# Two residual sums move from ScalarE and VectorE to VectorE alone, and their shifts into 32 columns

## The chip, the cores and the metric

The kernel runs on one core of one Trainium2 chip. The metric is device time in microseconds (us) from one launch to its end; lower is better.

## The reference

Eight layers in a row act on x of shape (8, 512, 128) in float32. Each layer has the form x = x + LN(layer(LN(x))), where LN takes mean and variance over the 128 channels of one token and has no weights. What matters here is the end of the sequence:

```python
x = x + _layernorm(_L2_ffn_ref(_layernorm(x), ...))    # expert choice
x = x + _layernorm(_L3_attn_ref(_layernorm(x), ...))   # rotary attention, 16 heads of 8
x = x + _layernorm(_L3_ffn_ref(_layernorm(x), ...))    # mixture of up to 4 experts
return x

def _layernorm(x, axis=-1, eps=1e-05):
    m = jnp.mean(x, axis=axis, keepdims=True)
    v = jnp.var(x, axis=axis, keepdims=True)
    return (x - m) / jnp.sqrt(v + eps)
```

LN of an output o is o times a scale plus a shift, where scale = 1/sqrt(var + eps) and shift = -mean times scale. Both are one number for each token. Adding one number to all 128 channels of a token doesn't change LN of that token.

## The kernel before

The 4096 tokens lie as 32 tiles of 128 tokens: a token is a partition, its 128 channels lie along the free axis. `c.x` holds the running sum, `c.n` the normalised input of the next layer, `c.o` the output of the last one. Four tiles make one of the 8 batches (`TPB` = 4, `B` = 8). The stages follow each other in the program (`program`), each a block with one instruction stream for each engine; the order within a stream is written out by hand, and engines wait for each other on semaphores.

A normalisation is an object of class `LayerNorm` with four steps, each of one batch:

- `spread` on VectorE (DVE): four BN_STATS (L2505) and four BN_AGGR (L2508) give mean and variance.
- `factors` on GpSimd (POOL): variance plus eps (L2514), minus the mean (L2515), the power -1/2 (L2517), the shift (L2520). Where the object has `late`, one more addition puts `c.late` on top of the shift (L2522, L2524).
- `apply` or `apply_tile` on ScalarE (ACT): one activation for each tile, scale times source plus shift (L2543, L2536).
- `add` on DVE: one SCALAR_TENSOR_TENSOR for each tile, x + o times scale, without the shift (L2530).

`c.late` is 32 columns, one for each tile. The stage before expert choice (linear attention) adds its two residuals by `add` and leaves the sum of the two shifts in `c.late`; the last normalisation of the mixture, `of_y`, adds it to its own shift, so the final x gets it.

The residual in front of a layer comes in two stages. In the rotary attention (`attention_layer` with `tables`, so `rope` is true) DVE runs `o_spread(b)`, POOL `of_o.factors`, ACT `of_o.apply` in place on `c.o`, and DVE `add(b)`, one TENSOR_TENSOR over 128x512 (L919). Then `x_spread(b)`, `of_x.factors` and `of_x.apply` give `c.n`. The mixture (`elastic_mixture`) does the same: `of_o.spread`, `of_o.factors`, `of_o.apply`, and `first_norm(b)` with its TENSOR_TENSOR (L2699) and the spread of x.

The attention's opening does batches 0 to 2 before the main loop. DVE: spreads of o(0) and o(1), `add(0)`, spread of x(0), weights copied, a memset (L985), spread of o(2), `add(1)`, spread of x(1), `add(2)`, spread of x(2), then two exchanges (STREAM_SHUFFLE, L931) and the splitting of queries into three bf16 parts (L509 to L515), which POOL does for the keys. ACT: `of_o.apply` of 0 and 1, `of_x.apply(0)`, copies `copy_tokens` (L814) and `keep` (L823), `of_o.apply(2)`, `of_x.apply(1)`, further copies. `keep(1, n)` waits for the parts of batch 0. POOL has the factors of o(0), o(1), x(0), two memsets (L646, L648), then the factors of o(2) and x(1).

The main loop has 32 quads of heads (i), each with four steps (k). In a step PE makes four score tiles (L740), the values of the step before (L750, eight matmuls), and two tiles for the row maxima (L727); ACT takes four exponentials (L839) and DVE two maxima (L942), from PSUM in both cases. Four quads belong to one batch (r = i mod 4), and the work for later batches is laid beside them: `of_x.apply_tile` at steps 1 to 4 of a batch, `of_o.apply_tile` at steps 5 to 8, `o_spread` on DVE at (r, k) = (0, 2), `add` at (2, 2), `x_spread` at (3, 2). PE makes keys at (2, 3) and values at (3, 3). These additions run for the five batches 3 to 7, on groups 0 to 4 of four quads.

In the mixture PE works through 32 pairs of batch and expert, `up` (L2608) and `down` (L2620); ACT does relu (L2656) and the two or three applies, DVE gathers (L2741).

Of the kernel before, what the change touches and what calls it, by code (L numbers as in the profile page):

```python
# [8 lines left out]
ALU = mybir.AluOpType  # L9
AX = mybir.AxisListType  # L10

B, S, D = 8, 512, 128
# [384 lines left out]
def attention_layer(c, tag, w, scale, tables=None, reload=None):  # L397
# [119 lines left out]
    with nc.Block() as block:  # L517
# [68 lines left out]
        def _(pool):  # L586
# [79 lines left out]
            for i in range(QUADS):  # L666
# [19 lines left out]
                if i + 2 < QUADS:  # L686
                    split_max(i + 2)

        @block.tensor
# [121 lines left out]
        def _(act):  # L811
# [45 lines left out]

            if rope:
                of_o.apply(act, c.o, c.o, 0)
                of_o.apply(act, c.o, c.o, 1)  # L860
            of_x.apply(act, c.n, c.x, 0)
            copy_tokens(0)
            keep(0, 0)
            keep(0, 1)
            if rope:
                of_o.apply(act, c.o, c.o, 2)
            of_x.apply(act, c.n, c.x, 1)
# [9 lines left out]
            for i in range(QUADS):  # L877
                b = i // TPB + AHEAD
                for k in range(4):
                    exps(i, k)  # L880
                    if k == 1 and i < LAST:
                        rows(i + 1)
                    at = 4 * (i % TPB) + k
                    if b < B and 1 <= at <= 4:
                        of_x.apply_tile(act, c.n, c.x, TPB * b + at - 1)
                    if rope and b + 1 < B and 5 <= at <= 8:
                        of_o.apply_tile(act, c.o, c.o, TPB * b + at - 1)
                    if b < B and at == 6:
                        copy_tokens(b)
                    if b < B and at == 7:  # L890
                        keep(b, 0)
                    if b < B and at == 11:
                        keep(b, 1)
                    if b < B and at == 15:
                        keep_values(b)

        @block.vector
        def _(dve):
# [18 lines left out]
            def add(b):  # L917
                dve.wait_ge(of_o.normed, TPB * (b + 1))
                nc.vector.tensor_tensor(batch_rows(c.x, b), batch_rows(c.x, b), batch_rows(c.o, b), ALU.add).then_inc(summed, 1)  # L919

            def x_spread(b):
                if rope:
                    dve.wait_ge(summed, b + 1)
                of_x.spread(dve, c.x, b)
# [1622 lines left out]
def elastic_mixture(c, d, small, out):  # L2547
# [15 lines left out]
    w1_in, w2_in, b1_turned, b1_copied = sem("w1_in"), sem("w2_in"), sem("b1_turned"), sem("b1_copied")  # L2563
    o_added, y_added, stored = sem("o_added"), sem("y_added"), sem("stored")
    turned, copied, gated, u_done, w_step, w_done = (sem(s) for s in ("turned", "copied", "gated", "u_done", "w_step", "w_done"))
# [5 lines left out]
    with nc.Block() as block:  # L2571
# [69 lines left out]
        def _(act):  # L2641
# [18 lines left out]
            nc.scalar.activation(b1T, c.bank(1)[:, 0:MIX * CHUNKS], ACT.Copy).then_inc(b1_copied, 1)  # L2660
            of_o.apply(act, c.o, c.o, 0)
            of_x.apply(act, c.n, c.x, 0)
# [4 lines left out]
            for g in range(STEPS):  # L2667
                b, e = divmod(g, MIX)
                if g + 1 < STEPS:
                    relu(g + 1)  # L2670
                if b + 1 < B and e == 0:
                    of_o.apply(act, c.o, c.o, b + 1)
                if b >= 1 and e == 0:
# [9 lines left out]
        @block.gpsimd  # L2683
        def _(pool):
            of_o.factors(pool, 0)
            of_x.factors(pool, 0)
            for b in range(B):
                if b >= 1:
                    of_y.factors(pool, b - 1)
                if b + 1 < B:  # L2690
                    of_o.factors(pool, b + 1)
                    of_x.factors(pool, b + 1)
            of_y.factors(pool, B - 1)

        @block.vector
        def _(dve):
# [4 lines left out]
            def first_norm(b):  # L2701
                residual(of_o, b, o_added)
                dve.wait_ge(o_added, b + 1)
                of_x.spread(dve, c.x, b)
# [160 lines left out]
```

## Time and profile before

| what | value |
|---|---|
| median of 3 runs | 2046.47 us |
| the 3 runs | 2046.47, 2047.84, 2041.81 us |
| the profiled execution, its own time | 2041.99 us |
| its span, first to last instruction | 2040.3 us |
| outside the span | 1.7 us |
| mean granted TensorE clock | 0.824 of 2.4 GHz |
| busy, of the span | PE 77%, DVE 60%, ACT 52%, POOL 39% |

In a row, a time is us from the start of the span; "x4" is the number of instructions; the part in brackets at the end is the engine's idle time just before and what ended it. Busy shares of the whole span are a mean over ten stages with different limits.

### The profile page before, as it was taken

Reading aid. Unit: us, or ns where it says so; the run is one execution under the profiler, and the core shown is the slowest. Engines: PE = TensorE matmul, PEld = TensorE weight load, DVE = VectorE, ACT = ScalarE, POOL = GpSimd, SP = SyncE. Lnnn points to the kernel's source line nnn. Section 1 sums busy time; section 2 is a strip of 40 time slices with the busy share of each in tenths; the row PEclk is TensorE's granted clock in tenths of the full one; section 3 lists DMA queues with packets and bytes.
Section 4 is the critical chain, followed back from the end, with each engine's and each line's share of the span. In section 5 each row is a group of like instructions: output and inputs, shape, how many; then the busy total and the mean of one; then the engine's idle time right before and its main releaser. Section 6 shows DMA issues by size and latency. Waiting matters only on the chain. (4 is left out here: it accounts for less than half of the span.)

```text
span 2040.3 us, 25722 instructions
## 1 busy us (share of the span) xinstructions
PE 1580.5 (77%) x8391; PEld 826.9 (41%) x8391; DVE 1224.0 (60%) x2794; ACT 1069.7 (52%) x2129; POOL 800.5 (39%) x1497
## 2 busy tenths in 40 slices
PE   2899999992659885074772595289999999789998
PEld 1133333320436554063662463123333333367776
DVE  3788888875743323004656750778888888334553
ACT  2377777774333333034663331257777777545553
POOL 3455555416243333515634376614444431011220
PEclk7699999996755555596765698579999999989999
DMA  4122222200000002100004122211111111000000
GB/s 117 66 66 66 65 67 64 64 14 1 1 0 1 0 1 88 54 28 10 3 1 129 55 39 30 90 48 60 61 62 59 61 64 45 26 18 11 11 6 16
DMA packets 84968, 85.16 MB, mean 42 GB/s; under 512 B 35942, under 2 KB 67536, under 8 KB 84708
## 3 DMA queue, kind: packets, MB, share of 16 engines
q1 hardware_dynamic: 73914, 75.14, 11.4%
q0 software_dynamic: 7680, 6.06, 1.8%
q10 hardware_dynamic: 3242, 2.32, 0.4%
q8 instruction: 67, 1.10, 0.2%
q14 instruction: 65, 0.53, 0.1%
HBM read 59.76 MB, written 25.17 MB: 42 GB/s over the span
## 5 line engine op out<-in xcount | busy, mean ns | idle before, releaser
L942 DVE TENSOR_REDUCE arena<-psum 128x2 f32<-128x1024 f32 x512 | 601.6, 1216 | 102.8 <-PE psum L727 98.3
L839 ACT ACTIVATE arena<-psum 128x512 f32<-128x512 f32 x1024 | 553.5, 595 | 135.4 <-PE psum L740 127.4
L727 PE MATMUL psum<-arena 72*128 72x512 bf16 x1024 | 287.8, 397 | 46.4 <-DMA arena<-L_k_parts 17.8
L740 PE MATMUL psum<-arena 99*128 99x512 bf16 x1024 | 312.0, 386 | 10.6 <-issue 7.1
L750 PE MATMUL psum<-arena 128*32 128x512 f32 x2048 | 274.5, 608 | 3.0 <-ACT arena L839 1.9
L2543 ACT ACTIVATE arena<-arena 128x128 f32<-128x128 f32 x316 | 128.6, 481 | 133.5 <-POOL arena L2520 121.3
L740 PEld LDWEIGHTS psum<-arena 99*128 99x128 bf16 x1024 | 74.6, 98 | 287.5 <-ACT arena L839 222.1
L2514 POOL TENSOR_SCALAR arena<-arena 128x4 f32<-128x4 f32 x112 | 30.6, 273 | 368.7 <-DVE arena L2508 363.2
L727 PEld LDWEIGHTS psum<-arena 72*128 72x128 bf16 x1024 | 95.3, 99 | 189.9 <-DVE arena L942 29.0
L2505 DVE BATCH_NORM_STATS2 arena<-arena 128x6 f32<-128x128 f32 x448 | 96.7, 278 | 75.9 <-PEq L101 21.0
L636 POOL TENSOR_TENSOR arena<-arena 128x16 bf16<-128x16 f32 x64 | 14.3, 223 | 290.8 <-DVE arena L942 218.4
L2656 ACT ACTIVATE arena<-psum,arena 128x512 f32<-128x512 f32 x128 | 84.3, 682 | 77.3 <-PE psum L2608 75.3
L627 POOL COPY arena<-arena 72x1024 f32<-72x1024 f32 x64 | 64.6, 1037 | 146.7 <-PE psum L740 126.5
L2620 PEld LDWEIGHTS psum<-arena 128*128 128x128 f32 x1024 | 118.1, 192 | 8.2 <-issue 8.2
L2517 POOL TENSOR_TENSOR arena<-arena 128x4 f32<-128x4 f32 x112 | 116.5, 1040 | 9.3
L2620 PE MATMUL psum<-arena 128*128 128x128 f32 x1024 | 119.9, 275 | 0.0
L2608 PE MATMUL psum<-arena 128*128 128x512 f32 x256 | 117.1, 601 | 0.0
L2741 DVE SCALAR_TENSOR_TENSOR arena<-psum,arena 128x128 f32<-128x128 f32 x128 | 36.0, 343 | 127.3 <-PE psum L2620 126.6
L750 PEld LDWEIGHTS psum<-arena 128*32 128x32 f32 x2048 | 40.4, 108 | 110.8 <-ACT arena L839 60.7
L2608 PEld LDWEIGHTS psum<-arena 128*128 128x128 f32 x256 | 46.9, 193 | 47.8 <-issue 47.8
L1741 POOL DMA_INDIRECT arena<-sw_rows_out,arena x32 | 33.2, 1037 | 67.8 <-SPq L1782 57.2
L1820 PE MATMUL psum<-arena 128*128 128x128 f32 x64 | 15.6, 392 | 55.3 <-ACT arena L2543 55.3
(433 smaller groups left out, 2532.2 us busy)
## 6 DMA issues: line engine op xcount, KB each, us to landing
arena<-L_q_parts SPq DMA_DIRECT2D x192, 96.0 KB
arena<-L_k_parts SPq DMA_DIRECT2D x180, 96.0 KB
L_q_parts<-arena SPq DMA_DIRECT2D x16, 384.0 KB, 3.4
L_k_parts<-arena SPq DMA_DIRECT2D x16, 384.0 KB, 3.3
arena<-in_L_ffn_w SPq DMA_DIRECT2D x1, 2048.0 KB, 10.6
ec_result<-arena SPq DMA_DIRECT2D x1, 2048.0 KB, 9.7
arena<-in_L_ffn_fc2s SPq DMA_DIRECT2D x1, 2048.0 KB, 16.1
ec_normed<-arena SPq DMA_DIRECT2D x2, 1024.0 KB, 7.3
```

Of the source, the lines that this page charges most:

```text
L627: nc.gpsimd.tensor_copy(rows[0:QK_ROWS, i % RING, :].rearrange("p (g j l) -> p g j l", g=4, j=HEADS), raw[0:QK_ROWS, i % RAW, :].rearrange ...
L727: last = nc.tensor.matmul(bank[:, 512 * h:512 * h + 512], columns(q9[0:QK_ROWS], i, m // 2, 128 * (2 * (m % 2) + h), 128), columns(k9[0:QK ...
L740: nc.tensor.matmul(acts.bank(name), columns(k9[0:ROWS], i, g, 128 * k, 128), columns(q9[0:ROWS], i, g, 0, 512), start=True, stop=True).the ...
L750: last = nc.tensor.matmul(out_bank[32 * g:32 * g + 32, :], v32[:, i % 2, g, k, :], prob[:, k % 2, g, :], start=(k == 0), stop=(k == 3))
L839: nc.scalar.activation(prob[:, k % 2, g, :], acts.bank(name), ACT.Exp, scale=scale).then_inc(act_taken, 1)
L942: nc.vector.tensor_reduce(neg_max[:, i % 2, 2 * m:2 * m + 2], maxes.bank(("max", i, m)).rearrange("p (h t) -> p h t", h=2), axis=AX.X, op= ...
L2505: self.nc.vector.bn_stats(self.stats[:, t, :], src[:, t, :]).then_inc(self.stats_done, 1)
L2517: self.nc.gpsimd.tensor_tensor(self.scale[:, at], self.var_eps[:, at], self.minus_half[:, 0:TPB], ALU.pow).then_inc(self.scale_done, 1)
L2543: self.nc.scalar.activation(dst[:, t, :], src[:, t, :], ACT.Identity, bias=self.shift[:, t:t + 1], scale=self.scale[:, t:t + 1]).then_inc( ...
L2608: nc.tensor.matmul(c.bank(k), w1[:, e, 128 * k:128 * k + 128], c.nT[:, b, 1:S + 1], start=True, stop=True).then_inc(h_made, 1)
L2620: last = nc.tensor.matmul(c.bank(4 + g % 2)[:, 128 * t:128 * t + 128], hT[:, g % 2, k, 128 * t:128 * t + 128], w2[:, e, k, :], start=(k == ...
L2656: nc.scalar.activation(hT[:, g % 2, k, :], c.bank(k), ACT.Relu, bias=b1T[:, CHUNKS * e + k:CHUNKS * e + k + 1]).then_inc(h_done, 1)
```

## The change

ACT no longer applies `of_o` in the rotary attention or the mixture. DVE's `add(b)` becomes `of_o.add`: four SCALAR_TENSOR_TENSOR of 128x128 in place of one TENSOR_TENSOR of 128x512, and it waits for POOL's factors where it waited for ACT. `c.x` then lacks the shift of that residual. POOL adds the shifts to `c.late`: once over 32 columns at the end of the attention, and in the mixture over 4 columns for each batch (`o_factors`, with a semaphore that `y_factors` waits for), ahead of the factors of `of_y`.

```diff
+            if rope:
+                pool.wait_ge(of_o.factors_done, B)
+                nc.gpsimd.tensor_tensor(c.late, c.late, of_o.shift, ALU.add)
...
-            if rope:
-                of_o.apply(act, c.o, c.o, 0)
-                of_o.apply(act, c.o, c.o, 1)
             of_x.apply(act, c.n, c.x, 0)
             copy_tokens(0)
             keep(0, 0)
             keep(0, 1)
-            if rope:
-                of_o.apply(act, c.o, c.o, 2)
             of_x.apply(act, c.n, c.x, 1)
...
-                    if rope and b + 1 < B and 5 <= at <= 8:
-                        of_o.apply_tile(act, c.o, c.o, TPB * b + at - 1)
...
             def add(b):
-                dve.wait_ge(of_o.normed, TPB * (b + 1))
-                nc.vector.tensor_tensor(batch_rows(c.x, b), batch_rows(c.x, b), batch_rows(c.o, b), ALU.add).then_inc(summed, 1)
+                of_o.add(dve, c.x, c.o, b, summed)
 
             def x_spread(b):
                 if rope:
-                    dve.wait_ge(summed, b + 1)
+                    dve.wait_ge(summed, TPB * (b + 1))
...
-            of_o.apply(act, c.o, c.o, 0)
             of_x.apply(act, c.n, c.x, 0)
...
-                if b + 1 < B and e == 0:
-                    of_o.apply(act, c.o, c.o, b + 1)
...
-            of_o.factors(pool, 0)
+            def o_factors(b):
+                at = slice(TPB * b, TPB * b + TPB)
+                of_o.factors(pool, b)
+                pool.wait_ge(of_o.factors_done, b + 1)
+                nc.gpsimd.tensor_tensor(c.late[:, at], c.late[:, at], of_o.shift[:, at], ALU.add).then_inc(late_summed, 1)
+
+            def y_factors(b):
+                pool.wait_ge(late_summed, b + 1)
+                of_y.factors(pool, b)
...
             def first_norm(b):
-                residual(of_o, b, o_added)
-                dve.wait_ge(o_added, b + 1)
+                of_o.add(dve, c.x, c.o, b, o_added)
+                dve.wait_ge(o_added, TPB * (b + 1))
                 of_x.spread(dve, c.x, b)
```

On DVE, the opening of the attention from `add(0)` on; before:

```order
L919 TENSOR_TENSOR arena<-arena 128x512
L2505 BN_STATS arena<-arena 128x6 x4
L2508 BN_AGGR arena<-arena 128x2 x4
L910 COPY arena<-arena 128x32 x8
L985 MEMSET arena 32x4096
L2505 BN_STATS arena<-arena 128x6 x4
L2508 BN_AGGR arena<-arena 128x2 x4
L919 TENSOR_TENSOR arena<-arena 128x512
L2505 BN_STATS arena<-arena 128x6 x4
L2508 BN_AGGR arena<-arena 128x2 x4
L919 TENSOR_TENSOR arena<-arena 128x512
```

The same place in the changed kernel, whose line numbers are 5 lower here:

```order
L2525 SCALAR_TENSOR_TENSOR arena<-arena 128x128 x4
L2500 BN_STATS arena<-arena 128x6 x4
L2503 BN_AGGR arena<-arena 128x2 x4
L906 COPY arena<-arena 128x32 x8
L980 MEMSET arena 32x4096
L2500 BN_STATS arena<-arena 128x6 x4
L2503 BN_AGGR arena<-arena 128x2 x4
L2525 SCALAR_TENSOR_TENSOR arena<-arena 128x128 x4
L2500 BN_STATS arena<-arena 128x6 x4
L2503 BN_AGGR arena<-arena 128x2 x4
L2525 SCALAR_TENSOR_TENSOR arena<-arena 128x128 x4
```

Nothing moved past anything else; each addition is now four instructions.

On ACT, the opening of the attention, before:

```order
L2543 ACTIVATE arena<-arena 128x128 x12
L814 ACTIVATE arena<-psum 128x512
L823 ACTIVATE arena<-psum,arena 128x512 x2
L2543 ACTIVATE arena<-arena 128x128 x8
L831 ACTIVATE arena<-psum 128x512
```

and now:

```order
L2538 ACTIVATE arena<-arena 128x128 x4
L817 ACTIVATE arena<-psum 128x512
L826 ACTIVATE arena<-psum,arena 128x512 x2
L2538 ACTIVATE arena<-arena 128x128 x4
L834 ACTIVATE arena<-psum 128x512
```

Eight applies ahead of x(0) and four ahead of x(1) are gone.

## Rows read from the trace of the kernel before

**Rows 1.** Stretches: length, busy PE, PEld, DVE, ACT, POOL, PEclk, DMA share, GB/s

```profile
1500.00:1525.00 25.00, 24.32 (x143) 8.13 (x135) 22.58 (x40) 18.96 (x38) 15.20 (x28) 1.00 0.19 65
...
1850.00:1875.00 25.00, 25.00 (x144) 18.04 (x143) 14.04 (x62) 13.18 (x26) 5.76 (x13) 1.00 0.04 11
```

**Rows 2.** The groups by line, attention's main loop (idle before and its releasers last)

```profile
L740 PE MATMUL psum<-arena 99*128 99x512 bf16 x490 | 147.8, 383 | 1.0 <-ACT arena L839 0.8
...
L727 PE MATMUL psum<-arena 72*128 72x512 bf16 x474 | 127.9, 379 | 8.1 <-DVE arena L973 7.0 <-DVE arena L942 1.1
```

**Rows 3.** The chain that ended last, the mixture's opening (start us, us, what)

```profile
1783.32 0.21 POOL arena L2520
...
1783.56 1.66 ACT arena L2543 x4
...
1785.96 0.88 DVE arena L2505 x4
```

**Rows 4.** The timeline of the attention's opening

```profile
1280.56 0.20 POOL L2520 TENSOR_TENSOR arena<-arena 128x4 f32<-128x4 f32 x1
...
1283.20 0.87 DVE L2505 BATCH_NORM_STATS2 arena<-arena 128x6 f32<-128x128 f32 x4
...
1292.47 0.38 DVE L2508 BATCH_NORM_AGGREGATE arena<-arena 128x2 f32<-128x6 f32 x4
...
1293.13 0.20 POOL L2520 TENSOR_TENSOR arena<-arena 128x4 f32<-128x4 f32 x1
...
1293.93 0.69 ACT L823 ACTIVATE arena<-psum,arena 128x512 f32<-128x512 f32 x1 [0.64 <-PE psum L701]
...
1296.90 0.87 DVE L2505 BATCH_NORM_STATS2 arena<-arena 128x6 f32<-128x128 f32 x4
...
1298.12 0.72 DVE L931 STREAM_SHUFFLE arena<-arena 128x512 f32<-128x512 f32 x1
...
1307.81 0.69 ACT L823 ACTIVATE arena<-psum,arena 128x512 f32<-128x512 f32 x1 [8.32 <-DVE arena L515]
...
1322.24 1.89 PE L727 MATMUL psum<-arena 72*128 72x512 bf16 x4 [17.83 <-DMA arena<-L_k_parts]
```

**Rows 5.** DVE's timeline in the linear attention stage, which has such additions already

```profile
925.50 1.14 DVE L2530 SCALAR_TENSOR_TENSOR arena<-arena 128x128 f32<-128x128 f32 x4 [2.10 <-POOL arena L2520]
926.67 0.87 DVE L2505 BATCH_NORM_STATS2 arena<-arena 128x6 f32<-128x128 f32 x4
```

**Rows 6.** DVE's timeline in the main loop, at an `add` and an `x_spread`

```profile
1490.72 0.68 DVE L919 TENSOR_TENSOR arena<-arena 128x512 f32<-128x512 f32 x1
1491.32 2.35 DVE L942 TENSOR_REDUCE arena<-psum 128x2 f32<-128x1024 f32 x2
...
1504.04 0.86 DVE L2505 BATCH_NORM_STATS2 arena<-arena 128x6 f32<-128x128 f32 x4
...
1505.23 2.32 DVE L942 TENSOR_REDUCE arena<-psum 128x2 f32<-128x1024 f32 x2
```

**Rows 7.** PE's timeline after the `x_spread`, with an `o_spread` ahead, and without

```profile
1507.69 1.03 PE L727 MATMUL psum<-arena 72*128 72x512 bf16 x4
...
1518.70 1.06 PE L750 MATMUL psum<-arena 128*32 128x512 f32 x8
...
1521.93 1.07 PE L750 MATMUL psum<-arena 128*32 128x512 f32 x8
...
1625.55 1.07 PE L750 MATMUL psum<-arena 128*32 128x512 f32 x8
...
1628.39 1.06 PE L750 MATMUL psum<-arena 128*32 128x512 f32 x8
```

**Rows 8.** The table of stretches, where PE starts the mixture

```profile
1790.00:1792.00 2.00, 0.98 (x4) 0.71 (x4) 0.00 (x0) 0.97 (x3) 1.24 (x2) 0.50 0.00 0
...
1796.00:1798.00 2.00, 2.00 (x3) 0.67 (x2) 1.93 (x8) 0.69 (x1) 0.00 (x0) 0.50 0.00 0
1798.00:1800.00 2.00, 2.00 (x5) 0.91 (x4) 1.96 (x8) 1.29 (x2) 0.00 (x0) 0.86 0.00 0
```

More of the change, by code:

```diff
@@ L2563, in elastic_mixture @@
     w1_in, w2_in, b1_turned, b1_copied = sem("w1_in"), sem("w2_in"), sem("b1_turned"), sem("b1_copied")
-    o_added, y_added, stored = sem("o_added"), sem("y_added"), sem("stored")
+    o_added, y_added, stored, late_summed = sem("o_added"), sem("y_added"), sem("stored"), sem("late_summed")
     turned, copied, gated, u_done, w_step, w_done = (sem(s) for s in ("turned", "copied", "gated", "u_done", "w_step", "w_done"))
@@ L2684, in _ @@
         def _(pool):
-            of_o.factors(pool, 0)
+            def o_factors(b):
[6 more added lines that the diff above has]
+                of_y.factors(pool, b)
+            o_factors(0)
             of_x.factors(pool, 0)
@@ L2688, in _ @@
                 if b >= 1:
-                    of_y.factors(pool, b - 1)
+                    y_factors(b - 1)
                 if b + 1 < B:
-                    of_o.factors(pool, b + 1)
+                    o_factors(b + 1)
                     of_x.factors(pool, b + 1)
-            of_y.factors(pool, B - 1)
+            y_factors(B - 1)
         @block.vector
```

## The prediction

> **What bounds the kernel now.** I read the page first, then the table of stretches over the two stages that the change touches, the groups by line and the waits of the attention's loop, the chain of waits for the mixture, and last the timelines of the two openings. The whole-span shares tell little, since ten stages differ. In a stretch of the attention's loop PE is busy for 24.32 of 25 us, DVE for 22.58 and ACT for 18.96; in a stretch of the mixture PE is busy for all 25.00 and DVE and ACT for 14.04 and 13.18 [rows 1]. So PE sets the pace of both loops. The groups say for whom it waits in the loop: the 490 score matmuls on ACT for 0.8 us in all, the 474 matmuls for the maxima on DVE for 7.0 and 1.1 us [rows 2]. ACT, which the change relieves, holds PE up for less than a microsecond in 400. DVE, which the change loads, is the one that PE does wait for. What neither row covers are the openings, before PE has work: there the path goes DVE, POOL, ACT, DVE, POOL, ACT, and the change takes one of the two ACT links out. The reader is to look for the gain there.
>
> **The mixture's opening.** The factors of o(0) end at 1783.53; ACT starts its four applies at 1783.56, DVE then adds, and the spread of x(0) starts at 1785.96 [rows 3], 2.40 us after 1783.56. In the changed kernel four SCALAR_TENSOR_TENSOR stand there. The linear attention stage has just these: four of them start 0.03 us after POOL's factors, take 1.14 us, and the spread of the sum starts 1.17 us after the first [rows 5]. So 2.40 becomes 1.17: **-1.23 us**. Everything up to PE's first transposes hangs on that chain, PE is then busy to the end, and the gain should reach the end whole.
>
> **The attention's opening.** Three additions lie there, and I go through it once.
> - Batch 0: factors end at 1280.76, ACT and DVE follow, the spread of x(0) starts at 1283.20 [rows 4]. With a start at 1280.79 that is 2.41 us, and it becomes 1.17: -1.24. POOL's factors of x(0), its memsets and the factors of o(2) queue up behind this, as do ACT's copies and DVE's memset; all come 1.24 earlier.
> - Batch 1: here ACT had long been done, so the addition only gets longer, from 0.70 (start to start) to 1.17. The spread of x(1) ends at 1292.85 now [rows 4]; it will end at 1292.85 - 1.24 + 0.47 = 1292.08.
> - Batch 2: the factors of o(2) end at 1293.33 [rows 4], so at 1292.09. Today ACT can't apply them at once: it is waiting in `keep` until 1294.62, and DVE, behind ACT, starts the spread of x(2) only at 1296.90 [rows 4]. Changed, DVE adds at 1292.12 and starts that spread at 1293.29: 3.61 us earlier. This is the largest term, and it comes less from the four activations than from where they stand in ACT's queue.
> - What is late next: DVE's first exchange (1298.12 now, so 1294.51) needs ACT's `keep(0, 0)`, which is done ahead of `keep(0, 1)`, and that one's end moves to 1294.62 - 1.24 = 1293.38, ahead of it. The second exchange comes later still. The splits follow on DVE and POOL, and `keep(1, 0)` waited 8.32 us for DVE's split of batch 0 [rows 4], so it follows DVE. From there to PE's first matmul for the maxima, which waited 17.83 us for the loads of keys [rows 4], the chain is splits, store and load. I take the whole **-3.61 us** through it. Its bounds are 0 (the DMAs end when they end) and -3.61.
>
> **The attention's loop.** Each of the five additions at (2, 2) goes from 0.60 us (1490.72 to 1491.32, when the next maximum starts [rows 6]) to at most 1.17. What 1.2 us of DVE at such a place costs PE can be read off twice. At (3, 2) `x_spread` holds the maxima back by 1.19 us [rows 6], beside extra PE work (the values of a batch), and PE's next matmuls for the maxima start without waiting for DVE: the row has no idle time ahead of it [rows 7]. The cost is 0. At (0, 2) `o_spread` is as long, with no extra PE work, and PE's step from one L750 to the next is 1521.93 - 1518.70 = 3.23 us, against 1628.39 - 1625.55 = 2.84 in group 5, where nothing is spread at (0, 2) [rows 7]: a cost of 0.39. The addition at (2, 2) is followed by the keys at (2, 3), like the values a projection of one batch, so it is like the first case. I take **0**; the bounds are 0 and 5 x 0.39 = +1.95.
>
> The 20 applies that ACT loses in the loop and the 28 in the mixture's loop (7 batches) are worth nothing: PE's waits for ACT were 0.8 us [rows 2] and none. Their cover is PE's own work. POOL's 8 small additions to `c.late` and the one over 32 columns lie where POOL has been idle for several us or is through with its stage; 0. The tail of the kernel (factors, apply and sum of the last batch) is unchanged, since `late` was added there before.
>
> **The sum** is -1.23 - 3.61 = -4.84 us, 0.24%. On the profiled execution that gives 2041.99 - 4.84 = 2037.15. That execution lies 4.5 us below the median of the three runs, close to the lowest of them, so against the median I say 2046.47 - 4.84 = **2041.6 us**. The runs spread by 6.0 us, and 0.3% (6.1 us) is about what a measurement of this kernel can tell from no change: the gain is just inside.
>
> **Rivals.**
> - A, the clock takes half back. PE begins the mixture at 1791.0 at the lower level, 1.2 GHz (0.50), and gets 2.4 GHz at about 1798.6 (0.50 until 1798, then 0.86 over 2 us) [rows 8]. If the rise stays at its own time while the work starts earlier, the time won is worked at 1.2 GHz and is worth half, in both openings: -2.42, so 2044.1. For it: nothing ties the rise to the first matmul in one trace. Against: PE had been at work without a break for some 6 us before it.
> - B, the clock gives more. If the rise comes after half of that stretch of 7.6 us, it gives 7.6 / 4 = 1.9 more at each of the two loop starts: -8.6, so 2037.8. The Trainium skill (TensorE: Matmul & The Clock Gate, What's actually happening) says that the window of the gate runs freely and that the transition point depends on where the first matmul lands in it. By that rule A and B are both open; one trace of before cannot show it.
> - C, DVE costs in the loop after all: the keys don't cover the addition, 0.39 x 5. 2046.47 - 4.84 + 1.95 = 2043.6. Rows 2 speak for it (PE waits for DVE, not for ACT), the step with the values against it.
> - D, slower. PE's gap at the five additions grows so far that the granted clock falls. Each fall would cost the gap of 0.39 and half of a stretch like the 7.6 us of rows 8, 4.2 together, 21 for five: 2046.47 - 4.84 + 21 = 2062.6. It decides from the point at which the gap brings the clock down; gaps of 0.2 to 0.4 us occur in every batch now, with the clock at 1.00 [rows 1], so it would take far longer ones.
>
> **How the numbers follow.** The forecast gets 0.57, A 0.12, C 0.12, B 0.15, D 0.04. B is faster by over 0.3% (8.6 us), and of the forecast's 0.57 I put 0.10 past that bound, as the medians scatter by a few us: faster 0.25. Same is the rest of the forecast with A and C: 0.71. Slower is D, 0.04. The range reaches from B with 2 us of scatter, 2036, to A with 3 us of scatter, 2047; D and the ends of the scatter are left out.
>
> **What would show it.** In the attention's opening of the changed profile, DVE's third addition starts at POOL's third factors and the first exchange comes 3.6 us earlier, counted from the first spread of o; PE's first matmul for the maxima as well. In the mixture 1.17 us lie between the first addition and the spread of x(0), and PE's first transpose comes 1.2 earlier, counted from the stage's start. PE's step after the addition at (2, 2) stays at 2.84 us; 3.2 would mean C. The stretches at clock 0.50 at both loop starts tell A and B. The prediction is wrong if PE's first maxima don't move with the exchange, if the step of rows 7 appears at five more places, or if a loop changes its length by more than 2 us.

## The result, and the profile after

| | the changed kernel | the kernel before |
|---|---|---|
| median | 2035.81 us (7 runs) | 2042.86 us (7 runs) |
| lowest to highest | 2033.16 to 2039.85 us | 2041.81 to 2047.84 us |
| the profiled execution's own time | 2033.53 us | 2041.99 us |
| ratio | 0.9965, 95% interval 0.995 to 0.998 | |

The change is faster by 7.05 us of the medians, 0.35%. I had said 4.84. The median lies 0.2 us below the range, whose lower end, 2036, was 2035.8 before I rounded it.

The page of the changed kernel, its span and its first part. The whole-span shares have hardly moved, as was to be expected:

```profile
span 2031.8 us, 25723 instructions
## 1 busy us (share of the span) xinstructions
PE 1576.3 (78%) x8391; PEld 822.3 (40%) x8391; DVE 1230.3 (61%) x2842; ACT 1047.9 (52%) x2065; POOL 799.4 (39%) x1506
```

Against [rows 1], the same two stretches, moved up by about the time by which they come earlier. The columns are the busy times of PE, PEld, DVE, ACT and POOL, each with its instructions, the granted clock, the DMA share and GB/s:

```profile
1495.00:1520.00 25.00, 24.32 (x143) 8.03 (x142) 22.55 (x38) 18.53 (x38) 13.39 (x26) 1.00 0.20 67
1841.00:1866.00 25.00, 25.00 (x147) 18.28 (x146) 14.51 (x65) 11.18 (x20) 5.88 (x14) 1.00 0.04 11
```

PE sets the pace of both loops as before; ACT has lost 2 us in the mixture's stretch, and PE is as busy as it was.

Against [rows 2], the groups of PE in the attention's loop (L743 is the score matmul, L730 the one for the maxima):

```profile
L743 PE MATMUL psum<-arena 99*128 99x512 bf16 x488 | 147.5, 383 | 1.5 <-DMA arena<-arena 0.7 <-ACT arena L842 0.5
...
L730 PE MATMUL psum<-arena 72*128 72x512 bf16 x476 | 128.3, 379 | 8.1 <-DVE arena L968 7.0 <-DVE arena L937 1.1
```

PE's waits for DVE are 7.0 and 1.1 us, exactly those of before: the longer additions have added none.

Against [rows 3], the chain of waits for the mixture's opening (start, length, what):

```profile
1775.84 0.21 POOL arena L2515
...
1776.07 1.18 DVE arena L2525 x4
...
1777.28 0.88 DVE arena L2500 x4
...
1786.00 9.10 PE psum L2603 x16
```

The link of ACT is gone; from the first addition to the spread of x(0) it is 1.21 us, where it was 2.40 from ACT's start. I had said 1.17.

Against [rows 4], the timeline of the attention's opening:

```profile
1275.79 0.20 POOL L2515 TENSOR_TENSOR arena<-arena 128x4 f32<-128x4 f32 x1
1276.03 1.14 DVE L2525 SCALAR_TENSOR_TENSOR arena<-arena 128x128 f32<-128x128 f32 x4 [0.92 <-POOL arena L2515]
...
1277.20 0.87 DVE L2500 BATCH_NORM_STATS2 arena<-arena 128x6 f32<-128x128 f32 x4
...
1284.87 1.11 DVE L2525 SCALAR_TENSOR_TENSOR arena<-arena 128x128 f32<-128x128 f32 x4
1285.15 0.39 POOL L2509 TENSOR_SCALAR arena<-arena 128x4 f32<-128x4 f32 x1
...
1285.62 0.44 POOL L2510 TENSOR_SCALAR arena<-arena 128x4 f32<-128x4 f32 x1
...
1287.49 1.14 DVE L2525 SCALAR_TENSOR_TENSOR arena<-arena 128x128 f32<-128x128 f32 x4 [0.19 <-POOL arena L2515]
...
1288.20 0.69 ACT L826 ACTIVATE arena<-psum,arena 128x512 f32<-128x512 f32 x1 [1.02 <-PE psum L704]
...
1289.88 0.72 DVE L926 STREAM_SHUFFLE arena<-arena 128x512 f32<-128x512 f32 x1
...
1314.39 1.89 PE L730 MATMUL psum<-arena 72*128 72x512 bf16 x4 [15.77 <-DMA arena<-L_k_parts]
```

The third addition starts at 1287.49, before ACT has begun the second half of `keep` (1288.20); before the change DVE stood behind it. DVE waits 0.19 us for POOL there, two of whose operations took 0.39 and 0.44 us beside the addition of batch 1.

Against [rows 6], DVE's timeline at an addition of the loop:

```profile
1483.37 1.13 DVE L2525 SCALAR_TENSOR_TENSOR arena<-arena 128x128 f32<-128x128 f32 x4
1484.42 2.35 DVE L937 TENSOR_REDUCE arena<-psum 128x2 f32<-128x1024 f32 x2
```

Against [rows 7], PE's timeline: two batches of the value product beside that addition, and two after a spread of o:

```profile
1485.55 1.07 PE L753 MATMUL psum<-arena 128*32 128x512 f32 x8
...
1488.38 1.06 PE L753 MATMUL psum<-arena 128*32 128x512 f32 x8
...
1511.36 1.06 PE L753 MATMUL psum<-arena 128*32 128x512 f32 x8
...
1514.58 1.06 PE L753 MATMUL psum<-arena 128*32 128x512 f32 x8
```

The addition takes 1.05 us of DVE instead of 0.60, and PE's step there is 2.83. After the spread of o it is 3.22, as it was.

The totals scatter by more than the change gives, so I timed stages from their own starts, in the profiles of both kernels: from DVE's first spread of o to its first exchange, to PE's first matmul for the maxima and to its first score; the loop from that score to the mixture's first matmul; and from there to the first matmul with a weight of the mixture ("up"). A mark that is a matmul is taken where its weight load starts if that comes first, up to 0.04 us before the matmul's own row.

| profile | DVE's first spread of o at | exchange | maxima | score | loop | up | up to the end |
|---|---|---|---|---|---|---|---|
| before | 1277.42 | 20.70 | 44.82 | 66.76 | 435.98 | 14.32 | 245.72 |
| changed | 1272.65 | 17.23 | 41.73 | 63.50 | 436.53 | 13.10 | 245.95 |
| changed less before | -4.77 | -3.47 | -3.09 | -3.26 | +0.55 | -1.22 | +0.23 |

The last row is the puzzle. From the attention's start on, the change gives -3.26, +0.55, -1.22 and +0.23, together -3.70; the other 4.77 us of this pair come from stages that it doesn't touch. **Theory**: the two terms are as I sized them, the loop costs nothing, and what the medians show above 4.84 is scatter of the stages ahead. **Rivals**: the change really gives 7 us or more, by a way I don't know, for which the relief of ACT in the loops was the first candidate; or the loop has a cost or a gain that the clock hides.

### The profile page after: what moved, and what is told of

Its sections match the earlier page's. It is cut to its first block and busy times, and to the rows that moved or that the text cites. A ratio compares the mean times of both kernels' runs of the same rounds, so it can differ in the third digit from the quotient of the medians.

```text
span 2031.8 us, 25723 instructions
## 1 busy us (share of the span) xinstructions
PE 1576.3 (78%) x8391; PEld 822.3 (40%) x8391; DVE 1230.3 (61%) x2842; ACT 1047.9 (52%) x2065; POOL 799.4 (39%) x1506
## 5 line engine op out<-in xcount | busy, mean ns | idle before, releaser
L937 DVE TENSOR_REDUCE arena<-psum 128x2 f32<-128x1024 f32 x512 | 601.9, 1217 | 102.7 <-PE psum L730 97.4
L743 PE MATMUL psum<-arena 99*128 99x512 bf16 x1024 | 311.5, 386 | 11.8 <-issue 6.9
L730 PE MATMUL psum<-arena 72*128 72x512 bf16 x1024 | 287.1, 396 | 42.9 <-DMA arena<-L_k_parts 15.8
L743 PEld LDWEIGHTS psum<-arena 99*128 99x128 bf16 x1024 | 74.4, 98 | 289.4 <-ACT arena L842 223.1
L2538 ACT ACTIVATE arena<-arena 128x128 f32<-128x128 f32 x272 | 111.3, 481 | 136.9 <-POOL arena L2515 120.1
L730 PEld LDWEIGHTS psum<-arena 72*128 72x128 bf16 x1024 | 95.0, 98 | 185.7 <-DVE arena L937 29.0
```

The lines of the kernel that those rows point to most:

```text
L730: last = nc.tensor.matmul(bank[:, 512 * h:512 * h + 512], columns(q9[0:QK_ROWS], i, m // 2, 128 * (2 * (m % 2) + h), 128), columns(k9[0:QK ...
L743: nc.tensor.matmul(acts.bank(name), columns(k9[0:ROWS], i, g, 128 * k, 128), columns(q9[0:ROWS], i, g, 0, 512), start=True, stop=True).the ...
L937: nc.vector.tensor_reduce(neg_max[:, i % 2, 2 * m:2 * m + 2], maxes.bank(("max", i, m)).rearrange("p (h t) -> p h t", h=2), axis=AX.X, op= ...
L2538: self.nc.scalar.activation(dst[:, t, :], src[:, t, :], ACT.Identity, bias=self.shift[:, t:t + 1], scale=self.scale[:, t:t + 1]).then_inc( ...
```

## The experiments

The first four ran on one chip, beside 35 runs of the kernel before: median 2041.3 us. Line numbers in what follows are those of each run's own kernel, so they differ by a few.

**The kernel before, unedited.** No edit.

> The kernel before, unedited, as a second profile and as a null. In the two traces at hand the attention starts (first spread of o) at 1277.42 us before and 1272.65 after the change, 4.8 us apart in stages that the change does not touch. Theory 'image' (the changed program runs the untouched stages faster, whatever the cause): the attention starts within 1 us of 1277.4 here, and the ratio is 1.000. Theory 'chance' (these stages scatter between executions): the start may lie anywhere between 1272 and 1279, the ratio is 1.000 within 0.002. Both expect 66.8 us from that start to the first score matmul, and 260.1 us from the start of the mixture to the end.

Measured: 2040.54 us (11 runs), ratio 0.9997 [0.9986, 1.0007]. Two measurements of one kernel agree within 0.1% when there are so many runs. Its attention starts at 1277.87, its exchange comes at 20.48, the first score at 67.32 where I expected 66.8, and from the mixture's start to the end it is 259.7 where I expected 260.1: the marks too scatter by some tenths. The kernel before had a median of 2046.47 in the three runs of the prediction, 2042.86 in seven, 2041.3 in these 35.

**The attention alone.** The mixture is the old one; against the changed kernel, one of the places:

```diff
...
 def first_norm(b):
-    of_o.add(dve, c.x, c.o, b, o_added)
-    dve.wait_ge(o_added, TPB * (b + 1))
+    residual(of_o, b, o_added)
+    dve.wait_ge(o_added, b + 1)
...
```

> The change in the rotary attention alone; the mixture as before. Theory 'openings': 63.5 us from the first spread of o to the first score matmul (3.3 less than before), the loop unchanged within 0.6, the mixture 260.1; total 3 to 3.6 us less than before, ratio 0.9984. Theory 'image': on top of this the stages ahead of the attention are 3 to 5 us shorter, ratio 0.996 to 0.997. Rival 'ACT': relief of ScalarE in the loop is worth something, so the loop from first score to the mixture's start is more than 0.6 us shorter.

Measured: 2035.34 us (11 runs), ratio 0.9983 [0.9973, 0.9993]. Exchange at 17.23, maxima 42.16, first score 64.12, loop 435.55, up 14.31.

**The mixture alone.** The attention is the old one; against the changed kernel, one of the places:

```diff
...
 def add(b):
-    of_o.add(dve, c.x, c.o, b, summed)
+    dve.wait_ge(of_o.normed, TPB * (b + 1))
+    nc.vector.tensor_tensor(batch_rows(c.x, b), batch_rows(c.x, b), batch_rows(c.o, b), ALU.add).then_inc(summed, 1)
...
```

> The change in the mixture alone; the attention as before. Theory 'openings': only the mixture is shorter, 1.0 to 1.2 us, at its opening, ratio 0.9994 to 0.9995. Theory 'image': the stages ahead of the attention are shorter too, total 4 us or more less.

Measured: 2039.97 us (12 runs), ratio 1.0000 [0.9989, 1.001]. Exchange 20.98, maxima 45.94, first score 67.91, loop 435.62, up 13.10. The stage shows its 1.22 us; the total can't, since 1.2 us is 0.06% and the interval is 0.1% to each side.

**The changed kernel again.** No edit.

> The changed kernel once more, for a second profile and runs beside those of e1 to e3 on one chip. 'openings' plus 'chance': ratio 0.9976 (4.8 us), attention start anywhere between 1272 and 1279. 'image': ratio 0.9965 again, attention start within 1 us of 1272.7.

Measured: 2034.76 us (11 runs), ratio 0.9975 [0.9965, 0.9984]; 0.9976 is what 4.84 us make. Exchange 17.22, maxima 42.95, first score 64.76, loop 438.75, up 13.11. With the three before it, it settles two things: each half of the change moves its own marks and no others; and the stages ahead come out in two ways for either kernel. DVE's first row of the attention, in the kernel before, the changed one, the changed one again, and the mixture alone (whose stages up to here are those of before):

```profile
1277.42 0.87 DVE L2505 BATCH_NORM_STATS2 arena<-arena 128x6 f32<-128x128 f32 x4 [19.53 <-DMA arena<-ec_result]
```

```profile
1272.65 0.87 DVE L2500 BATCH_NORM_STATS2 arena<-arena 128x6 f32<-128x128 f32 x4 [19.62 <-DMA arena<-ec_result]
```

```profile
1277.35 0.87 DVE L2500 BATCH_NORM_STATS2 arena<-arena 128x6 f32<-128x128 f32 x4 [19.84 <-DMA arena<-ec_result]
```

```profile
1272.38 0.87 DVE L2505 BATCH_NORM_STATS2 arena<-arena 128x6 f32<-128x128 f32 x4 [19.68 <-DMA arena<-ec_result]
```

So the 4.77 us of the first pair of profiles are no effect of the change, and the theory 'image' is out: the changed program has here started its attention at 1277.35, as late as the kernel before. In all 14 profiles the mark lies at 1272.0 to 1274.0 or at 1276.4 to 1278.4.

The next four ran on another chip, beside 20 runs of the kernel before: median 2040.4 us.

**The opening alone.** The additions of the loop go back to ACT's apply and the plain sum; those of batches 0 to 2 stay as changed:

```diff
 def add(b):
-    of_o.add(dve, c.x, c.o, b, summed)
+    if b <= AHEAD:
+        of_o.add(dve, c.x, c.o, b, summed)
+    else:
+        dve.wait_ge(of_o.normed, TPB * (b - AHEAD))
+        nc.vector.tensor_tensor(batch_rows(c.x, b), batch_rows(c.x, b), batch_rows(c.o, b), ALU.add).then_inc(summed, TPB)
...
```

The mixture is the old one, `c.late` takes the shifts of three batches, and ACT has its `apply_tile` in the loop again.

> The new addition only for batches 0 to 2, in the attention's opening; for batches 3 to 7 ScalarE applies and VectorE adds 128x512 as before, and the mixture is as before. Theory 'openings': 17.2 us from the first spread of o to the first exchange, as in the changed kernel (20.5 to 21.0 before), 63.5 to 64.8 to the first score; the loop from first score to the mixture 435.5 to 436.5; total 3 to 3.6 less than before. Rival 'loop': the five additions in the loop bring or cost something of their own, so this kernel differs from e2 by over 1 us in the loop beside the waits for the rows' DMA.

Measured: 2036.5 us (10 runs), ratio 0.9984 [0.9973, 0.9995], the same as with the whole attention changed. Exchange 17.22, maxima 41.75, first score 63.60, loop 435.37. The loop is 0.2 us from that with the whole attention changed (435.55), which is within its scatter: the loop's part of the change neither costs nor gives anything that shows.

**ACT keeps its work.** DVE adds as in the changed kernel; ACT still does its 32 applies of the attention, into a tile that nobody reads:

```diff
+            if rope:
+                of_o.dead(act, scratch, c.o, 0)
+                of_o.dead(act, scratch, c.o, 1)
             of_x.apply(act, c.n, c.x, 0)
...
+                    if rope and b + 1 < B and 5 <= at <= 8:
+                        of_o.dead_tile(act, scratch, c.o, TPB * b + at - 1)
```

> The changed kernel, but in the attention ScalarE still does all 32 applies at their old places in its queue, into columns that nobody reads; VectorE doesn't wait for them. Theory 'the wait': what paid was that VectorE no longer waits for ScalarE, not the time ScalarE is relieved of. 17.2 us to the first exchange, and 63.5 to 64.8 to the first score, as in the changed kernel; the applies of x(1) come up to 0.7 us later, without effect; the loop unchanged. Rival 'relief': ScalarE's own time counts; then the first score comes up to 2 us later and the loop is longer by up to 20 x 0.4 = 8 us.

Measured: 2034.13 us (5 runs), ratio 0.9964 [0.995, 0.9978]. ACT's timeline of its opening, with the dead applies (L2545) at their old places:

```profile
1292.05 0.69 ACT L827 ACTIVATE arena<-psum,arena 128x512 f32<-128x512 f32 x1 [0.95 <-PE psum L705]
1292.63 1.64 ACT L2545 ACTIVATE arena<-arena 128x128 f32<-128x128 f32 x4
```

and DVE's first exchange, which starts while the four applies of batch 2 are still at work:

```profile
1293.78 0.72 DVE L934 STREAM_SHUFFLE arena<-arena 128x512 f32<-128x512 f32 x1
```

Exchange 17.23, maxima 42.31, first score 64.13, loop 434.72. The marks lie within those of the other profiles with the new additions, and the loop is no longer, so ACT's relief is worth nothing that shows; what gains is that DVE no longer waits for it. This rules out the relief of ACT as a way to 7 us.

**The loop's additions twice.** A second set of four into an unread tile behind each of the five additions at (2, 2):

```diff
...
                         add(b)
+                        for t in range(TPB):
+                            nc.vector.scalar_tensor_tensor(scratch[:, t, :], c.o[:, TPB * b + t, :], of_o.scale[:, t:t + 1], c.n[:, t, :],
+                                                           op0=ALU.mult, op1=ALU.add)
```

> The changed kernel with each of the five additions in the attention's loop done twice, the second time into columns that nobody reads: about 2.05 us of VectorE at (2, 2) in place of 1.03. An o_spread of 1.2 us costs PE 0.39 where nothing covers it, so a step has 0.8 us of room; the keys add 0.86; 1.66 in all. Theory 'cover': PE loses 2.05 - 1.66 = 0.4 us at each, 2 us in all, at the step behind the addition, and nothing more; the clock stays at 1.00. Rival 'no room': the first addition already used up the room, so the second costs its full 1.0 each, 5 us. Rival 'clock': the gaps bring the granted clock down and it costs 10 us or more.

Measured: 2036.24 us (10 runs), ratio 0.9978 [0.9968, 0.9988]. DVE's and then PE's timeline at the doubled place (lines are one higher):

```profile
1482.96 1.13 DVE L2529 SCALAR_TENSOR_TENSOR arena<-arena 128x128 f32<-128x128 f32 x4
1484.01 1.13 DVE L1015 SCALAR_TENSOR_TENSOR arena<-arena 128x128 f32<-128x128 f32 x4
1485.06 2.35 DVE L938 TENSOR_REDUCE arena<-psum 128x2 f32<-128x1024 f32 x2
```

```profile
1485.14 1.06 PE L754 MATMUL psum<-arena 128*32 128x512 f32 x8
...
1487.46 0.61 PE L731 MATMUL psum<-arena 72*128 72x512 bf16 x2 [0.28 <-DVE arena L938]
...
1488.43 1.06 PE L754 MATMUL psum<-arena 128*32 128x512 f32 x8
```

The step is 1488.43 - 1485.14 = 3.29 us, 0.46 more than 2.83, and it is so at all five places. In the table of PE's waits in the loop:

```profile
PE psum L731 <- DVE arena L938: 2.5, 10, 0.3
```

Ten waits instead of five. One addition fits under PE's work and a second doesn't: by the step, the cover is about 2.1 - 0.46 = 1.6 us of DVE, where I had worked out 1.66. 0.46 x 5 = 2.3 us is what the second costs in the steps, and not the 5 of the rival without room; neither the total nor the loop as a whole (436.44) is sharp enough to show them.

**The spread of o one group later.** Not in the change, but opened by it. Before, ACT's four applies of a batch followed the factors at steps 5 to 8, so the spread had to be at (0, 2). Without them only the addition at (2, 2) waits:

```diff
-                    if rope and b < B and (r, k) == (0, 2):
+                    if rope and b < B and (r, k) == (1, 2):
                         o_spread(b)
```

> The changed kernel with o_spread in the attention's loop moved from (0, 2) to (1, 2), in front of the queries' projection at (1, 3). Theory 'cover': PE's step of 3.22 us in row 0 becomes 2.83 in the five batches and no other step grows: the loop is 2.0 us shorter (433.6 to 434.6 from first score to the mixture, without late row DMAs), ratio 0.9965. Rival 'handed on': VectorE is late by the same amount at (1, 3) or (2, 0), and the loop keeps its length.

Measured: 2031.94 us (4 runs), ratio 0.9957 [0.994, 0.9973]; loop 434.43. Of PE's five waits for the maxima's DVE (L937, 1.1 us), one of 0.2 us is left. The first rows of the table of PE's waits are now:

```profile
PE psum L730 <- DVE arena L968: 7.1, 29, 0.2
...
PE psum L743 <- ACT arena L842: 1.3, 5, 0.3
```

All five steps of 3.22 us are 2.83: 0.39 x 5 = 1.95 us. The group has additional work of PE, the queries' projection, and that is what covers the spread; the time isn't handed on to a later step.

The next two ran on a third chip, beside 12 runs of the kernel before: median 2042.13 us.

**The opening reordered as well.** The later spread; in addition POOL makes the factors of o(2) and x(1) ahead of its memsets, and the memset of DVE (3.47 us) goes to ACT, behind its copies of batch 1:

```diff
...
             of_x.factors(pool, 0)
+            if rope:
+                of_o.factors(pool, 2)
+                of_x.factors(pool, 1)
             nc.gpsimd.memset(v32[:, :, :, :, HD:32], 1.0).then_inc(k_pads, 1)
...
```

> Kernel e8 with the attention's opening reordered, which is possible now that no addition waits for ScalarE: VectorE's memset of the queries' pad rows goes to ScalarE, behind copy_tokens(1), where it idles for 6 us, and POOL makes the factors of o(2) and x(1) ahead of its two memsets. Theory 'openings': VectorE is through with x(2) by 12.8 us and the second exchange then waits for keep(0, 1), at 16.2 us after the first spread of o; the split starts 1.5 us earlier than in the changed kernel, and so do the first maximum (40.3 to 41.4) and the first score (62.0 to 63.0). Loop as in e8. Ratio about 0.995. Rival 'DMA': the loads of keys and the DMA of the first row maxima end when they end, and the first score stays at 63.5 to 64.8.

Measured: 2034.45 us (6 runs), ratio 0.9963 [0.995, 0.9976]. Exchange at 14.76 instead of 17.23; both exchanges wait for ACT, now the late engine, the first for 1.87 us:

```profile
1292.33 0.72 DVE L931 STREAM_SHUFFLE arena<-arena 128x512 f32<-128x512 f32 x1
...
1294.04 0.01 DVE L931 LOAD_MASK_SELECT arena<-arena  x1 [0.99 <-ACT arena L828]
```

The split starts 1.4 us earlier (17.07 instead of 18.47), and PE's first matmul for the maxima at 40.93, where the ten other profiles with the new additions in this opening have 41.73 to 42.95. So the mark moves by about the 1.4 us of the split. The first score comes at 62.90, as expected, where those ten have 63.50 to 64.76. The total doesn't show it.

**The later spread again**, beside it.

> Kernel e8 once more, beside e9 on the same chip, so that the two can be set against each other and the median of e8 rests on more runs. Every theory: row 0 of the loop again without the step of 3.22 us, ratio 0.9957 to 0.997.

Measured: 2033.53 us (6 runs), ratio 0.9961 [0.9946, 0.9975]; first score 63.55, loop 433.36; no step of 3.22 us is left.

The last two ran beside 23 runs of the kernel before, median 2038.92 us: **the changed kernel**, and **the later spread a third time**.

> The changed kernel once more, on the chip and in the rounds of the next run. Theory (the stages timed from their own starts carry 4.8 us, the rest of a total is scatter of the stages ahead of the attention): about 4.8 us below the kernel before on the mean of the runs, ratio 0.9976, between 0.996 and 0.999. PE's waits for the maxima's DVE stand at 1.1 us, five times. Rival (the first comparison's 7 us are real): ratio 0.9965 or less.

> The changed kernel with the spread of o one group later, on the same chip. Theory (five steps of PE go from 3.22 to 2.83 us, and nothing else changes): 1.95 us below the changed kernel of the same call, so about 6.8 us below the kernel before, ratio 0.9967; the five waits of 1.1 us are gone from the profile. Rival (the two earlier runs of it, 0.9957 and 0.9961, show a larger gain than the steps carry): over 3 us below the changed kernel.

Measured: the changed kernel 2036.4 us (12 runs), ratio 0.9983 [0.9972, 0.9993], where 7 us would have been 0.9965; the later spread 2032.51 us (12 runs), ratio 0.9967 [0.9956, 0.9979], the ratio expected. Against the changed kernel beside it, the later spread is ahead by 3.9 us of the medians and 3.2 of the means, 2032.9 against 2036.1. I can place 1.95, and for the rival I had set over 3: taken by its letter the rival came. With 12 runs a side that spread by 7 to 9 us, each mean is known to some 0.8 us and their difference to 1.1, so the two can't be told apart, and whether the later spread gives more than its steps stays open. That it beats both kernels is shown, by the mean of all its 22 runs too: 2033.0 us against 2036.1 and 2040.7. The loop shows the place: it takes 434.2 us on the mean of the four profiles with the later spread, and 435.75 in those without (that of 438.75, of which below, left out).

## Why the prediction was right or wrong

**The base was wrong, and the scatter.** The steps that failed are the two sentences in which I chose the median of three, 2046.47, as the base and put the scatter at 2 to 3 us. I had seen that the profiled execution lay 4.5 us below it. Of the 5.8 us between the forecast and the measured median, 3.6 are the base (2046.47, where seven runs gave 2042.86) and 2.2 are what the medians gained above 4.84. The median fell next to the range's lower end, which came from rival B; B didn't happen, so had it fallen just inside, that would have been luck. The kernel before, over all five comparisons, has a mean of 2040.7 us in 97 runs, from 2036.1 to 2047.8. All three runs that I had lie in its upper part, as do all seven of the first comparison (2041.81 and above), although 13 of the 35 later ones lie below 2040. Against its own profile I had 2037.15; against 2040.7 it would have been 2035.9.

**The gain was right.** The changed kernel has a mean of 2036.1 us in its 30 runs, 4.6 below, each mean known to about 0.3 and 0.5; I had said 4.84. Its three ratios are 0.9965, 0.9975 and 0.9983, the forecast is 0.9976. The 7.05 us of the first comparison are that gain and some 2.4 us more, which lie with the kernel before: its seven runs there have a mean of 2043.9 us and its 90 others 2040.4, while the changed kernel has 2036.0 in its seven there and 2036.1 in its 23 others. Why those seven were slow, by chance or not, no run shows.

Term by term:

- **Mixture's opening, -1.23.** Measured -1.22 at "up", in every profile with the change (13.10 to 13.12 against 14.30 to 14.32). From there to the end the kernel takes 0.2 longer in this pair, so it isn't quite whole at the end. Over all 14 profiles that length is 245.5 us on the mean of the four with the old mixture (245.4 to 245.8) and 246.0 on that of the ten with the new one (245.6 to 246.5). What goes with it is the clock, of which below: some 0.4 of the 1.22 us may be lost again behind "up", where I had it reach the end whole.
- **Attention's opening, -3.61.** Measured -3.47 at the first exchange. The 0.14 that lacks stand in POOL's factors of o(2): they start 1.33 us earlier, counted from the first spread of o, but their four operations take 2.31 us to the last end instead of 2.08; DVE waits 0.19 us for them at the third addition. By the mechanism that I quoted from the Trainium skill (GPSIMD Engine Reference, Key points), GpSimd and VectorE contend for their SBUF interfaces. POOL's first two operations on the factors of o(2) take 0.39 and 0.44 us beside the new addition of batch 1. In the kernel before only the first lay beside the old one, which was shorter:

```profile
1291.25 0.37 POOL L2514 TENSOR_SCALAR arena<-arena 128x4 f32<-128x4 f32 x1
1291.70 0.23 POOL L2515 TENSOR_SCALAR arena<-arena 128x4 f32<-128x4 f32 x1
```

  So the first was lengthened before as well (with neither addition beside it, at 1278.80, it took 0.25), and the second is lengthened now: 0.44 in all ten profiles with the new additions in this opening, 0.22 to 0.23 in the three with the old. The trace agrees with the page's rule so far, and the price here is 0.2 us, where I had 0.5 as the most, without a working. Two inputs aren't the whole of it: beside the copies of the weights (L906), which have one, POOL's first operation on x(0) took 0.47 to 0.65 us in all of them. No run takes the addition away from beside these factors and leaves all else, so the cause is argued, not shown. The rest of the chain went as I had followed it: DVE's third addition is ahead of `keep`'s second half, and ACT holds up nothing.
- **That the whole of it passes through the splits, store and load.** PE's first matmul for the maxima comes at 44.82 to 45.94 and at 41.73 to 42.95, the first score at 66.76, 67.32 and 67.91 in the three profiles with the old attention, and at 63.50 to 64.76 in the ten with the new one (the reordered opening apart). The means, 67.3 and 64.1, differ by 3.3. It passes whole within that scatter: up to the exchange the new opening has 17.22 to 17.25, and behind the splits, store and loads the marks scatter by some 0.6 to each side.
- **The loop, 0.** PE's step at the addition is 2.83. Rival C is out: its 3.2 appeared only when the addition was doubled, at 0.46 a place, where I had 0.39 from [rows 7]. The reading of [rows 7], that a projection of one batch covers 1.2 us of DVE, is shown from both sides, by the doubled addition and by the later spread.
- **ACT's relief, 0.** Shown for the attention by the dead applies; for the mixture's loop no run tests it.
- **Rivals A and B, the clock.** At the attention's start neither came as a result of the change. I read off how long PE still works at 0.50 after the first score: 7.2 us before, 6.9 changed; over 13 of the 14 profiles 5.7 to 7.4, in no order of kernels. The fourteenth is the changed kernel again, the one with the loop of 438.75, with 12.3:

```profile
1346.00:1350.00 4.00, 4.00 (x14) 0.79 (x13) 1.26 (x2) 2.06 (x4) 0.00 (x0) 0.50 0.02 4
1350.00:1354.00 4.00, 4.00 (x14) 0.60 (x12) 2.36 (x2) 1.80 (x5) 0.00 (x0) 0.50 0.01 3
1354.00:1358.00 4.00, 4.00 (x25) 1.32 (x22) 2.68 (x5) 2.94 (x7) 0.00 (x0) 0.95 0.00 0
```

Its first score is at 1342.13 and PE is busy for all of these stretches. In the first profile of the same kernel the score is at 1336.19, and the stretches read:

```profile
1340.00:1344.00 4.00, 4.00 (x16) 0.78 (x14) 1.54 (x3) 2.01 (x4) 0.00 (x0) 0.62 0.01 4
1344.00:1348.00 4.00, 4.00 (x24) 1.22 (x27) 3.25 (x3) 3.55 (x9) 0.00 (x0) 1.00 0.01 3
```

The other thirteen have 6.4 us at the lower level on the mean. Half of 12.3 - 6.4 is 2.9 us, and this loop is 3.0 us longer than the mean of the nine others without the later spread, 435.75, more than the 2 us that I had set as a sign of being wrong. So the clock does take and give at this place, by chance and not by the change. The Trainium skill (TensorE: Matmul & The Clock Gate, What's actually happening) lets the point of the rise depend on where the first matmul falls, and gives that half a microsecond to either side. The 5.7 to 7.4 us scatter in that way but by more, and nothing in the page or the runs explains the 12.3.

  At the mixture's start it is less clear. The changed kernel's stretches against [rows 8], where PE starts at 1782.33 instead of 1791.02:

```profile
1788.00:1790.00 2.00, 2.00 (x3) 0.72 (x3) 1.97 (x8) 1.02 (x2) 0.00 (x0) 0.50 0.00 0
1790.00:1792.00 2.00, 2.00 (x6) 0.82 (x5) 1.33 (x5) 1.33 (x3) 0.00 (x0) 0.96 0.00 0
```

  From PE's first transposes to the rise it is 7.5 us before and 7.8 now. Over the profiles it is 6.8 to 7.7 in the four with the old mixture, 7.2 on the mean, and 7.2 to 8.9 in the ten with the new one, 7.9 on the mean. The length from "up" to the end goes with it: where the rise comes 3.3 us after "up" it is 245.4 us, where it comes 5.3 after, 246.5. That leans towards A in a small measure. The two ranges overlap, and nothing holds the rise fixed, so it isn't shown.
- **Rival D.** The clock stayed at 1.00 in the loop, even with the additions doubled.

**What stays open.** Why the stages ahead of the attention come out in two ways. Most of it arises in the test-time learner, where PE is idle for a good part: with ACT's instructions put one by one beside those of its first profile, the changed kernel again is 0.2 us ahead at 720 us, 3.0 behind at 760 and 4.5 at 1000. One late profile, that of the later spread again, is 2.6 us behind by 100 us already. Two profiles of the same changed kernel, the one with the early attention first:

```profile
700.00:732.00 32.00, 27.64 (x106) 20.01 (x106) 9.65 (x49) 11.10 (x31) 8.19 (x17) 0.55 0.00 1
732.00:760.00 28.00, 23.16 (x96) 17.66 (x95) 7.64 (x36) 9.37 (x26) 9.45 (x18) 0.56 0.00 1
```

```profile
700.00:732.00 32.00, 27.85 (x101) 20.61 (x101) 9.52 (x49) 11.10 (x31) 8.21 (x17) 0.50 0.00 1
732.00:760.00 28.00, 24.13 (x90) 17.79 (x89) 6.80 (x30) 9.38 (x26) 9.46 (x18) 0.50 0.00 1
```

The early one has PE at the higher level for about a tenth of that time, the other not at all. But the kernel before, a late one, also has 0.56 in the second of these stretches, so this is a thing that goes with it and not a proven cause. Summed over all that stands ahead of the attention, by the clock's own records, PE is at the lower level for 595 to 602 us in the four earliest profiles, 612 in the next two and 606 to 626 in the eight late ones. That goes the same way, with one exception (the 606); no run here holds the clock fixed.

## What to carry to other kernels

Where an engine that is on the path waits for another that applies a factor, look at what the other's queue holds at that moment, not at how busy it is. ACT's applies were worth 1.2 us in an opening where its queue was empty, 3.5 in one where the third of them stood behind a `keep`, and nothing that showed in the attention's loop, which PE bounds. A pass that is taken out also takes a deadline with it: here the spread of o could move to a place where PE's own work covers it, which by its steps gave 1.95 us more, 0.4 of what the openings had given, for one number in the source.

A gain of 0.2% is found in a stage timed from its own start, by one profile; in the totals it took some 30 runs. Behind DMAs even such a mark scatters, here by some 0.6 us to each side. Take as base all that is known of the kernel, its profiled execution too, not the median of three runs.

## What the runs showed of the hardware

- The totals of the kernel before spread over 6.0 to 10.1 us within a comparison and 11.7 over all 97 runs, 0.3 to 0.6%. In the comparison of 35 runs they lie in two heaps, 13 from 2037.3 to 2039.2 and 22 from 2040.8 to 2044.9; in those of 20 and 23 runs some lie between. The granted clock leans the same way and overlaps: 0.826 to 0.831 in the lower heap, 0.824 to 0.829 in the upper.
- PE, busy practically without a break from the attention loop's first score on, went from 1.2 to 2.4 GHz (granted clock 0.50 to 1.00) 5.7 to 7.4 us after it in 13 profiles, and once after 12.3.
- Two small operations of POOL took 0.29 to 0.42 and 0.44 us where four SCALAR_TENSOR_TENSOR of DVE ran beside both (batch 1, ten profiles), 0.37 to 0.50 and 0.22 to 0.23 where a shorter TENSOR_TENSOR ran beside the first (three profiles), 0.25 and 0.23 beside neither; beside copies of 128x32 on DVE the first took 0.47 to 0.65. Four such additions of 128x128 take 1.13 us to their end and 1.05 to the start of the next instruction, in place of 0.60 for the sum in one piece.
